# Channel norms from batch norm statistics of interleaved groups, and a relative bound for the row scan's residual

## The reference

```python
def _ln_c(v, eps=1e-06):
    m = jnp.mean(v, axis=-1, keepdims=True)
    s = jnp.var(v, axis=-1, keepdims=True)
    return (v - m) / jnp.sqrt(s + eps)
# _ln_t is the same with eps=1e-05
x = x + _L0_conv_ref(_ln_c(x), ...)   # triangle product with gates
t = t + _L0_ffn_ref(_ln_t(t), ...)    # routed experts over segments, top 8
x = x + _L1_conv_ref(_ln_c(x), ...)   # triangle product with gates and mask
t = t + _L1_ffn_ref(_ln_t(t), ...)    # batch norm, then a recurrence in time with a sigmoid
x = x + _L2_conv_ref(_ln_c(x), W)     # rows in sequence: row i = row i + relu(conv of row i-1's result)
t = t + _L2_ffn_ref(_ln_t(t), ...)    # as L1_ffn
x = x + _L3_conv_ref(_ln_c(x), ...)   # triangle product with gates
t = t + _L3_ffn_ref(_ln_t(t), ...)    # top 2 of 8 experts per token
```

## Time and profile before

| | |
|---|---|
| median of 3 runs | 665.69 us |
| profiled execution, whole | 664.4 us |
| its span, first to last instruction | 662.6 us |
| busy: PE, DVE, ACT, POOL | 461.7, 424.8, 286.3, 250.3 us |
| instructions | 8339 |
| mean granted TensorE clock | 0.83 of full speed |

### The profile page before, as it was taken

How to read it: one execution, slowest core, us unless ns; L and a number is a source line. 1 busy time by engine, 2 the same in 40 slices (tenths; PEclk the granted TensorE clock), 3 DMA queues, 4 the chain that set the end, 5 groups by cost and what they waited for, 6 DMA issues and landing times.

```text
span 662.6 us, 8339 instructions
## 1 busy us (share of the span) xinstructions
PE 461.7 (70%) x3015; PEld 358.8 (54%) x3015; DVE 424.8 (64%) x829; ACT 286.3 (43%) x658; POOL 250.3 (38%) x310
## 2 busy tenths in 40 slices
PE   2788744799476774798369983798389736738775
PEld 1457642578243653398349972498256625615443
DVE  6796459533958579601954469501958595499996
ACT  2776535601475455565460015566379544000000
POOL 1893554100467158200050003200359376045563
PEclk9999965876689785899859996989579975559999
DMA  6000000000000000000000000000000000001212
GB/s 203 1 1 1 1 1 0 0 1 0 1 0 1 1 0 2 0 1 1 1 0 1 1 2 1 0 1 1 1 0 1 1 1 0 1 0 29 36 30 35
DMA packets 19576, 6.01 MB, mean 9 GB/s; under 512 B 17068, under 2 KB 19244, under 8 KB 19501
## 3 DMA queue, kind: packets, MB, share of 16 engines
q1 hardware_dynamic: 19534, 5.46, 3.6%
HBM read 3.36 MB, written 2.10 MB: 8 GB/s over the span
## 4 chain that ended last, share of the span: by engine, by line
PE 41%; DVE 35%; POOL 10%; issue 8%; ACT 5%; DMA 1%; DVEq 0%; SPq 0%; POOLq 0%
PE psum L1242 6%; DVE stats L279 5%; POOL z L1513 5%; PE psum L1003 4%; DVE ab L647 4%; PE psum L1002 4%; PE psum L506 4%; PE psum L386 4%; PE psum L536 4%; DVE stats L282 3%; DVE z L292 3%; DVE stats L286 2%; PE psum L1385 2%; PE psum L1024 2%; ACT z_t L318 2%
## 5 line engine op out<-in xcount | busy, mean ns | idle before, releaser
L333 POOL TENSOR_TENSOR z<-z,stats 128x496 f32<-128x496 f32 (+1 forms) x64 | 79.2, 1238 | 177.2 <-DVE stats L289 177.2
L386 PE MATMUL psum<-ident,z 128*128 128x128 f32 x256 | 59.2, 377 | 77.8 <-POOL z L333 75.6
L386 PEld LDWEIGHTS psum<-ident,z 128*128 128x128 f32 x256 | 41.1, 192 | 108.0 <-POOL z L333 74.7
L506 PE MATMUL psum<-wp_L,z_t 64*128 64x320 f32 x384 | 65.9, 482 | 11.9 <-DVE tmp L647 6.4
L309 ACT ACTIVATE squares<-z 128x512 f32<-128x512 f32 x64 | 40.3, 630 | 57.5 <-DVE z L292 57.3
L506 PEld LDWEIGHTS psum<-wp_L,z_t 64*128 64x128 f32 x384 | 37.8, 202 | 35.6 <-issue 29.4
L1513 POOL TENSOR_TENSOR z<-gate 128x512 f32<-128x512 f32 x31 | 39.1, 1282 | 30.1 <-DVE gate L1488 30.1
L1095 ACT ACTIVATE ab<-psum,mv 128x128 f32<-128x128 f32 x112 | 41.1, 367 | 19.5 <-PE psum L1003 9.0
L318 ACT ACTIVATE z_t<-psum 128x512 f32<-128x512 f32 x56 | 39.7, 715 | 21.3 <-PE psum L386 21.1
L1003 PE MATMUL psum<-ab,R_vt 128*128 128x128 f32 x224 | 48.5, 300 | 0.0
L1002 PE MATMUL psum<-z_t,wbnt 128*128 128x128 f32 x224 | 46.4, 291 | 0.8 <-DVE wbnt L1148 0.8
(11 more groups left out here) (243 smaller groups left out, 1029.0 us busy)
## 6 DMA issues: line engine op xcount, KB each, us to landing
x_rows<-in_x_dram SPq DMA_DIRECT2D x4, 512.0 KB, 6.9
out_dram<-x_cols SPq DMA_DIRECT2D x32, 64.0 KB, 1.9
par<-in_par_dram SPq DMA_DIRECT2D x1, 644.5 KB
w<-in_w_dram SPq DMA_DIRECT2D x1, 264.0 KB
w<-in_w_dram SPq DMA_DIRECT2D x1, 256.0 KB
mask<-in_mask_dram SPq DMA_DIRECT2D x1, 64.0 KB
row<-in_row_dram SPq DMA_DIRECT2D x1, 3.3 KB
w2l<-in_w2l_dram SPq DMA_DIRECT2D x1, 2.0 KB
```

Source lines behind the costliest of these rows:

```text
L333: pool.tensor_tensor(Z4[:, r, :, 0:last_c], Z4[:, r, :, 0:last_c], rstd, ALU.mult).then_inc(L.s["z"], 1)
L386: m = pe.transpose(bank(b % 2)[:, k * N:(k + 1) * N], block_of(Z)(4 * b + k), ident[:, :])
L506: m = pe.matmul(bank(slot_bank(s) + h, 2 * 5 * C), ZT[rows, s, :], wp[l][rows, :, :], start=True, stop=True)
```

## The change

The norm's mean and variance now come from batch norm statistics. For each slice and each pair of groups, DVE issues one `bn_stats` over 64 numbers, read so that the two groups alternate. The instruction keeps statistics of the elements at even and at odd places apart (count, mean, count times variance), so one instruction gives both for two tokens a partition. Eight of them make a block. The results go to a new tile `moments`. The sums, the scaling to a mean, ACT's squares and the sums of squares are gone. ACT takes the root from `moments` directly. DVE takes the reciprocal and subtracts the mean one step behind the statistics, and POOL multiplies in that same step; before, the reciprocal and the multiplication came three steps behind the sums. The norm has Q + LAG = 10 steps instead of 12. Where a constant 1 is the last channel, DVE centres 31 channels.

F0's last products go to PSUM banks 2 to 5 instead of 0 to 3 and wait for three more weight copies, since those banks held weights. The row scan compares its residual, partition by partition, with SCAN_TOL = 2^-21 times the largest absolute state kept: one more reduction and one scaling on DVE, placed in the second round of steps, and one more product with the identity on PE, so that the flag compares the difference of the two with zero.

```diff
@@ -66,6 +66,7 @@
 FIXED_TOL = 2.0 ** -22
+SCAN_TOL = 2.0 * FIXED_TOL
 PAR = {}
...
@@ -127,6 +128,7 @@
         stats = sb("stats", [N, 4, N])
+        moments = sb("moments", [N, Q, SQ * G, 3])
         ident = sb("ident", [N, N])
...
@@ -255,7 +257,11 @@
         def ln_parts():
-            return [stats[:, k, :].rearrange("p (q s g) -> p q s g", q=Q, g=G) for k in range(4)]
+            return [stats[:, k, :].rearrange("p (q s g) -> p q s g", q=Q, g=G) for k in (0, 3)]
+        def ln_moment(q, k):
+            return moments[:, q, :, k].rearrange("p (s g) -> p s g", g=G)
         def over_c(t):
...
@@ -265,49 +271,45 @@
-        LN_STEPS = Q + LAG + 2
+        LN_STEPS = Q + LAG
+        def last_channel(L):
+            return C - 1 if "one" in L.s else C
         def ln_dve_step(dve, L, u):
             X4 = by_block(L.src) if L is sc else blocks(L.src).rearrange("p g s c -> p s g c")
-            Z4, SQ4 = by_block(Z), by_block(SQR)
-            SUM, MEAN, SS, RSTD = ln_parts()
-            q, before, first = u, u - LAG, u - LAG - 1
+            Z4 = by_block(Z)
+            STD, RSTD = ln_parts()
+            q, before = u, u - 1
             if 0 <= q < Q:
                 wait_all(dve, L.ready[q])
-                r = slice(SQ * q, SQ * (q + 1))
-                dve.tensor_reduce(SUM[:, q], X4[:, r], AX.X, ALU.add).then_inc(L.s["sum"], 1)
+                for s in range(SQ):
+                    for g in range(0, G, 2):
+                        k = s * G + g
+                        m = dve.bn_stats(moments[:, q, k:k + 2, :].rearrange("p k m -> p (k m)"),
+                                         X4[:, SQ * q + s, g:g + 2, :].rearrange("p g c -> p c g"))
+                m.then_inc(L.s["moments"], 1)
             if 0 <= before < Q:
-                dve.wait_ge(L.s["square"], L.at["square"] + before + 1)
-                dve.tensor_reduce(SS[:, before], SQ4[:, SQ * before:SQ * (before + 1)], AX.X, ALU.add)\
-                    .then_inc(L.s["sumsq"], 1)
+                r, c = slice(SQ * before, SQ * u), last_channel(L)
+                dve.wait_ge(L.s["std"], L.at["std"] + before + 1)
+                dve.reciprocal(RSTD[:, before], STD[:, before]).then_inc(L.s["rstd"], 1)
+                dve.wait_ge(L.s["moments"], L.at["moments"] + before + 1)
+                dve.tensor_tensor(Z4[:, r, :, 0:c], X4[:, r, :, 0:c],
+                                  ln_moment(before, 1).unsqueeze(3).to_broadcast([N, SQ, G, c]), ALU.subtract)\
+                    .then_inc(L.s["centred"], 1)
+        def ln_act_step(act, L, u):
+            STD, _ = ln_parts()
+            q = u
             if 0 <= q < Q:
-                dve.wait_ge(L.s["sum"], L.at["sum"] + q + 1)
-                dve.tensor_scalar(MEAN[:, q], SUM[:, q], 1.0 / C, None, ALU.mult).then_inc(L.s["mean"], 1)
-            if 0 <= first < Q:
-                dve.wait_ge(L.s["std"], L.at["std"] + first + 1)
-                dve.reciprocal(RSTD[:, first], SUM[:, first]).then_inc(L.s["rstd"], 1)
-            if 0 <= q < Q:
-                dve.wait_ge(L.s["mean"], L.at["mean"] + q + 1)
-                dve.tensor_tensor(Z4[:, r], X4[:, r], over_c(MEAN[:, q]), ALU.subtract).then_inc(L.s["centred"], 1)
-        def ln_act_step(act, L, u):
-            Z4, SQ4 = by_block(Z), by_block(SQR)
-            SUM, _, SS, _ = ln_parts()
-            q = u - LAG
-            if 0 <= q < Q:
-                act.wait_ge(L.s["sumsq"], L.at["sumsq"] + q + 1)
-                act.activation(SUM[:, q], SS[:, q], ACT.Sqrt, bias=eps[:, L.eps:L.eps + 1],
+                act.wait_ge(L.s["moments"], L.at["moments"] + q + 1)
+                act.activation(STD[:, q], ln_moment(q, 2), ACT.Sqrt, bias=eps[:, L.eps:L.eps + 1],
                                scale=(1.0 + L.e2) / C).then_inc(L.s["std"], 1)
...
                     warm_table(act, L.function)
-            q = u
-            if 0 <= q < Q:
-                r = slice(SQ * q, SQ * (q + 1))
-                act.wait_ge(L.s["centred"], L.at["centred"] + q + 1)
-                act.activation(SQ4[:, r], Z4[:, r], ACT.Square).then_inc(L.s["square"], 1)
-            q = u - LAG - 2
+            q = u - LAG
             if 0 <= q < Q:
...
@@ -318,19 +320,16 @@
         def ln_pool_step(pool, L, u):
-            q = u - LAG - 1
+            q = u - 1
             if 0 <= q < Q:
-                Z4, r = by_block(Z), slice(SQ * q, SQ * (q + 1))
-                pool.wait_ge(L.s["square"], L.at["square"] + q + 1)
-                last_c = C
+                Z4, r, c = by_block(Z), slice(SQ * q, SQ * (q + 1)), last_channel(L)
+                pool.wait_ge(L.s["centred"], L.at["centred"] + q + 1)
                 if "one" in L.s:
-                    last_c = C - 1
-                    pool.memset(Z4[:, r, :, last_c:], 1.0).then_inc(L.s["one"], 1)
+                    pool.memset(Z4[:, r, :, c:], 1.0).then_inc(L.s["one"], 1)
                 pool.wait_ge(L.s["rstd"], L.at["rstd"] + q + 1)
-                rstd = ln_parts()[3][:, q].unsqueeze(3).to_broadcast([N, SQ, G, last_c])
-                pool.tensor_tensor(Z4[:, r, :, 0:last_c], Z4[:, r, :, 0:last_c], rstd, ALU.mult).then_inc(L.s["z"], 1)
+                _, RSTD = ln_parts()
+                pool.tensor_tensor(Z4[:, r, :, 0:c], Z4[:, r, :, 0:c],
+                                   RSTD[:, q].unsqueeze(3).to_broadcast([N, SQ, G, c]), ALU.mult).then_inc(L.s["z"], 1)
         def ln_dve(dve, L):
...
@@ -831,14 +830,14 @@
             pe.wait_ge(L.s["outm"], L.at["outm"] + 1)
-            for V in (t1, t3):
-                pe.wait_ge(V.s["w_dve"], V.at["w_dve"] + TRI_W)
+            for V, count in ((t1, TRI_W), (t3, TRI_W), (f3, 2), (r1, 1), (r2, 1)):
+                pe.wait_ge(V.s["w_dve"], V.at["w_dve"] + count)
             for b in range(SEGI // 2):
...
                     i = 2 * b + k
-                    m = pe.matmul(bank(b % 4)[:, k * SEG * C:(k + 1) * SEG * C], WGT[:, i * N:(i + 1) * N],
+                    m = pe.matmul(bank(2 + b % 4)[:, k * SEG * C:(k + 1) * SEG * C], WGT[:, i * N:(i + 1) * N],
                                   outm[:, :, :], start=True, stop=True)
...
@@ -1111,11 +1110,11 @@
                 pool.memset(chunks(Y, CHUNK - WARM, h), 0.0).then_inc(L.s[f"step_y{h}"], 1)
-        def set_flag(dve, L, differences):
+        def set_flag(dve, L, differences, bound):
             dve.wait_ge(L.s["chk_ps"], L.at["chk_ps"] + 1)
...
             dve.wait_ge(L.s["flag"], L.at["flag"] + 1)
-            dve.tensor_scalar(flag_i[:, :], flag_f[:, :], FIXED_TOL, None, ALU.is_gt).then_inc(L.s["flag"], 1)
+            dve.tensor_scalar(flag_i[:, :], flag_f[:, :], bound, None, ALU.is_gt).then_inc(L.s["flag"], 1)
         def rec_dve(dve, L, after):
...
@@ -1258,8 +1257,10 @@
             turn_rows(1).then_inc(L.s["y_ps"], 1)
+            pe.wait_ge(L.s["size"], L.at["size"] + 2)
+            pe.matmul(bank(1)[0:1, 0:GC], mv[:, 11:12], ident[:, :], start=True, stop=False)
             pe.wait_ge(L.s["chk"], L.at["chk"] + 2)
-            pe.transpose(bank(1)[0:1, 0:GC], mv[:, 10:11], ident[:, :]).then_inc(L.s["chk_ps"], 1)
+            pe.matmul(bank(1)[0:1, 0:GC], mv[:, 10:11], ident[:, :], start=False, stop=True).then_inc(L.s["chk_ps"], 1)
             turn_rows(2).then_inc(L.s["y_ps"], 1)
...
@@ -1305,6 +1306,12 @@
                         row_step(first + k, h).then_inc(L.s[f"row{h}"], 1)
+                    if r == 1 and k == 1:
+                        dve.tensor_reduce(mv[:, 11:12], kept.rearrange("p k n -> p (k n)"), AX.X, ALU.max,
+                                          apply_absolute_value=True).then_inc(L.s["size"], 1)
+                    if r == 1 and k == 2:
+                        dve.wait_ge(L.s["size"], L.at["size"] + 1)
+                        dve.tensor_scalar(mv[:, 11:12], mv[:, 11:12], -SCAN_TOL, None, ALU.mult).then_inc(L.s["size"], 1)
             dve.wait_ge(L.s["row0"], L.at["row0"] + STEPS + 1)
...
@@ -1312,7 +1319,7 @@
             dve.tensor_reduce(mv[:, 10:11], differ, AX.X, ALU.max, apply_absolute_value=True).then_inc(L.s["chk"], 1)
-            set_flag(dve, L, bank(1)[0:1, 0:GC])
+            set_flag(dve, L, bank(1)[0:1, 0:GC], 0.0)
             for h in range(STREAMS):
```

More of the change, by code:

```diff
@@ L183, in build @@
         families = {
-            "norm": "sum:8 mean:8 centred:8 square:8 sumsq:8 std:8 rstd:8 z:8",
+            "norm": "moments:8 std:8 rstd:8 centred:8 z:8",
             "turn": "zt_ps:8 zt:8",
@@ L222, in build @@
         v1 = stage("V1", "turn_x", src=XC, dst=XR)
-        sc = stage("SC", "norm turn", "pads w_dve w_pool conv row0 row1 kept chk chk_ps flag g_conv g_row0 g_row1 g_turned"
+        sc = stage("SC", "norm turn", "pads w_dve w_pool conv row0 row1 kept size chk chk_ps flag g_conv g_row0 g_row1 g_turned"
                    " y_ps done", src=XR, eps=2, e2=0.0)
@@ L947, in f0_dve @@
                     x = xi[:, 2 * b + k]
-                    i = dve.tensor_tensor(x, x, bank(b % 4)[:, k * SEG * C:(k + 1) * SEG * C]
```

(1 more changed line is left out.)

2 lines of the change are left out of this document (1 added, 1 removed).

## The result

The changed kernel took 635.52 us (median of 4 runs, 632.19 to 636.94), the kernel before 665.61 beside it: a ratio of 0.954, 95% interval 0.950 to 0.958. The forecast was 654.9 with a range of 641 to 664, so it was wrong: the gain is 30.1 us where 10.8 were expected. The profiled execution took 635.63 (span 633.8), 28.8 less than that of before. Its runs spread by 5 us, so differences under about 3 us are read from rows, not from times.

What follows compares the result with a forecast made beforehand. No engine was taken to bound the whole, so each of eight norms was read alone. Gains in L0, F0, T1, R1, SC, R2, T3 and F3 summed to 10.95, less 0.2 for the scan: 10.8 us, hence 654.9, range 641 to 664.

Steps and rivals of the forecast that it cites:

- (a): Norm statistics: eight bn_stats a block at 0.17 us each, 1.36, replace 1.26 us of DVE and ACT's square (0.63).
- The low end: Statistics price at contiguous cost: 64/0.96 GHz plus about 0.06, 0.127 us each, 1.02 a block.
- The high end: Statistics price if short bn_stats don't overlap at all: 0.255 us each, 2.04 a block.
- Rival 1: Statistics at 0.127 us; centring plus POOL bound a pure-norm block at 1.86 to 1.92; 644 us in all; chance 18%.
- (b): Pure norms, worked out on F0: first z at 3.7 us, last at 19.0, table load hidden; F0 gains 1.5.
- (c): Ends of R2 and R1, where PE needs banks freed by DVE's bn_stats: gains 1.1 and 0.8 us.
- (d): Joint steps of R1 and F3: new serial chain of 4.1 us a step for 3.86; F3 gains 2.5.
- (e): T3: five steps of 2.72 us, the fifth z at 479.7 instead of 482.9; gain 2.3.
- (f): Scan check: added reduction and scaling hidden in DVE's idle time, added matmul costs up to 0.2 us; 0.2 charged.
- Rival 4: Scan's residual check trips and the general scan runs: 150 us more, 805 us; chance 1%.
- Rival 2: Short bn_stats don't overlap, 0.255 us each: 689 us; chance 14%, with what lies between 0.20 and 0.255.
- Rival 3: PE's clock falls to 1.2 GHz in gaps: 5 us in R2, as much in R1, 2 in F0; 660 to 666; 14%.

Runs made afterwards that it cites:

- u1: Changed kernel plus nine rows of sixteen back-to-back VectorE instructions at its program's end: statistics 0.127 us each with two streams, 0.167 with four; no total time given.
- e1: Changed kernel plus one further statistics instruction over 256 elements a block, making a block's statistics 1.35 us: 652.95 us, ratio 0.980.
- e3: Changed kernel with reciprocal and centring two steps later in F0, SC and R2, VectorE's work unchanged: 638.35 us, ratio 0.961.
- e5: Changed kernel with ScalarE's copies of the turned z one step later in R1 and F3: 631.07 us, ratio 0.946.
- the second measurement: The changed kernel itself, unedited, measured again beside other experiments: 634.22 us, ratio 0.953.
- e7: Changed kernel with the scan's old check (one transpose, no maximum over kept states) and a fixed bound 64 times as wide: 634.15 us, ratio 0.953.

## Why the prediction was wrong

**The step that failed is (a), the price of a statistics instruction.** It took 0.17 because L414 was called the nearest row; the price is 0.127, 1.02 a block for 1.36. u1 shows the row to be of another kind: four streams, where the edit reads two. Putting the price back (e1) brings 18.7 us, against 19.4 between the forecast and the measured time. That the rest is so small is luck, since smaller errors cancel: with the price restored the norms still win 14.6 where 10.95 were reckoned, the most in T3 and F3 (3.5 and 3.6 for 2.3 and 2.5), and R2 nothing for 1.1; but 5.0 are lost between the norms, 2.6 of them from R1's to SC's. Part of the norms' surplus is the centring, 0.545 from start to start for the 0.60 that was taken, about 0.4 a norm.

The low end was worked out in the same paragraph from bn_stats' own rows (64/0.96 + 0.06 = 0.127) and was exact. The same sum by the Trainium skill's 58+FD cycles (VectorE: DVE Perf Modes, its errata section) gives that value too, and the trace agrees if it is read from start to start: 0.127. Its section "The DRAIN you can't avoid" also says that an operation that is not held starts earlier, and that is what the trace shows: statistics that last 0.21 start 0.127 apart. The high end did not follow from that section.

**Rival 1 had the right price and the wrong floor.** It put centring plus z at 0.69 + 0.14 + 1.03 = 1.86 to 1.92 a block, hence 644. Measured are 0.63, 0.09 to GpSimd and 1.05, less 0.04 by which the next centring starts early: 1.73, no more than VectorE's own sum of 1.02 + 0.155 + 0.545. The 0.14 was read from a reciprocal's end to a z that started beside a centring and lasted 1.33. The 0.69 is the length of the old centrings that met no work of GpSimd; why the new one lasts 0.63 no run shows. 0.13 to 0.19 a block, eight blocks in six norms, would be 6 to 9 us, enough for rival 1's miss of 8.5; no run takes it alone.

**(b), the end of F0.** Table load before the last z, right (108.28 to 109.56). First z 2.92 after the start for 3.7 forecast, last z 15.98 for 19.0: most of both is the price (two blocks are 0.67, eight 2.7). e3 shows that the shorter chain as such brings little: with the longer delay and the same work the three norms lose 4.2 to 5.5 in all, part of it by centrings that meet a z.

**(c) and (d), R1 and R2.** The chain centring, z, L712, L717 came as foretold, 3.90 for 4.1, and R1's gain was 1.1 for 0.8. That is half luck: the root behind a waiting copy on ScalarE was not seen, and it held back 2.6 us (e5). The distance between root and copy on ScalarE is what it was, but the copies are issued two steps earlier, now before the banks are free for which TensorE's first product waits, with a block's turn behind it. The prediction followed the queues of VectorE and GpSimd and did not go through ScalarE's. It also read the old centring of 1.64 as ending with the L718 beside it; its rows have it end at 261.25, 0.56 behind L718, as the new ones do. R2's gain was 2.9 (4.2 in u1) for 1.1: VectorE turns to the statistics that free TensorE's banks 15.2 after the start (13.8 in u1) for 17.1, and the price alone is 2.7. F3's was 4.0 for 2.5, of which the price is 0.4 (e1); joint steps of 3.90 for 4.1 give a little more, and the rest was not traced.

**(e), T3.** A step was 2.31 for 2.72 forecast and 2.60 before; 0.41 in eight steps is 3.3 of the 4.1 missed; e1 gives 2.8 of it to the price.

**(f), the scan.** 0.2 was forecast and 0.42 is what the check costs; the reduction and the scaling are hidden, as said. The scan itself took 39.97 in one execution of the changed kernel and 39.12 in the second measurement's (39.13 before): in the first its second and third intervals between row steps are 1.28 and 1.00 where the others have 0.77 and 0.67, and TensorE's granted clock there is 0.50 to 0.52 (330 to 334) where the second has 0.95 after its first steps. In u1 and e7, with the clock as in the first, these two intervals are 1.28 and about 1.00 too. So of the 1.6 lost there 0.85 goes with that clock, 0.42 is the check's and 0.3 stays open. Why the clock rose later was not tried. Rival 4's mechanism exists, but only with the old bound (828 for 805 forecast): 224 steps at 0.86, where 0.67 was taken.

**Rivals 2 and 3.** Rival 2's price didn't occur; its arithmetic was sound (692.4 for 689). Rival 3, a lower clock in the tails of R2 and R1, did not come in the changed kernel, though the waits did: after 1.72 of waiting TensorE's product takes 1.10, as in the earlier trace rows. Its mechanism is real all the same: in e1 a wait of 1.67 in R2's tail was followed by the lower level. That it stayed out at the new price was not to be known from the rows of before.

## What to carry to other kernels

When the cost of an access pattern is read from another line, match the number of streams, the operation and the count of elements; if an end of the range comes from the operation's own rows, that end deserves the weight. Before an engine is counted as free for moved work, look at what its neighbour does in the rows where they meet: here 2 x 0.545 taken off VectorE's work in a norm came back in longer centrings. When a chain gets shorter, go through every in-order queue for an instruction that now waits in front of one that others need. When two executions of one kernel differ by more than an effect, look where the granted clock differs before a row is charged to the edit. And an edit that changes rounding can reach a comparison far away: try the halves of such a change alone.
